# Cross attention on one Trainium2 core: the row order of the key and query stacks, and the weight columns that feed them

## The reference, cut to what matters

```python
qh = (layernorm(x) @ Wq + bq)      # 256 x 256, split into 16 heads of 16
kh = (ctx @ Wk + bk)
vh = (ctx @ Wv + bv)
attn = softmax(qh @ kh.T * scale)  # per sequence and head, 256 x 256
x = x + (attn @ vh) @ Wo + bo
```

## Time and profile before

| | |
|---|---|
| median of 3 runs | 2549.36 us |
| the profiled execution, its own time | 2551.32 us |
| its span | 2549.6 us |
| mean granted clock of PE | 0.945 of full |
| PE busy | 2233.4 us, 88% of the span |
| DVE / ACT / POOL busy | 1249.1 / 1044.1 / 690.6 us |
| DMA packets | 110,836, of them 95,256 under 2 KB |
| bytes moved | 164.30 MB |
| stack DMAs (lines 590 and 606) | 144 + 144 of 128 KB |
| L0x, L2x, L3x start at | 4.6, 1334.8, 2013.3 us |

### The profile page before, as it was taken

How to read it: one execution, slowest core, us unless ns; L and a number is a source line. 1 busy time by engine, 2 the same in 40 slices (tenths; PEclk the granted TensorE clock), 3 DMA queues, 4 the chain that set the end, 5 groups by cost and what they waited for, 6 DMA issues and landing times. The chain is left out here.

```text
span 2549.6 us, 43063 instructions
## 1 busy us (share of the span) xinstructions
PE 2233.4 (88%) x13610; PEld 1651.1 (65%) x13611; DVE 1249.1 (49%) x2762; ACT 1044.1 (41%) x2555; POOL 690.6 (27%) x684
## 2 busy tenths in 40 slices
PE   8998398668898999898898998999997599879998
PEld 4664398434465874466785664679996356558887
DVE  4664300379776229876434664100000466567864
ACT  1664133213565433466532663134443046544332
POOL 1000200337522436621541000320001410044443
PEclk8999699789999999999998998999998789999999
DMA  7761143110000000000007741133221476100001
GB/s 183 160 168 69 49 166 111 40 42 0 26 0 15 26 17 0 25 0 4 11 10 143 126 78 73 40 116 106 72 105 51 102 154 125 33 26 20 25 26 34
DMA packets 110836, 164.30 MB, mean 64 GB/s; under 512 B 15272, under 2 KB 95256, under 8 KB 105720
## 3 DMA queue, kind: packets, MB, share of 16 engines
q1 hardware_dynamic: 101712, 140.68, 21.6%
q0 software_dynamic: 7680, 20.98, 2.7%
q10 hardware_dynamic: 1320, 1.03, 0.2%
HBM read 114.96 MB, written 47.32 MB: 64 GB/s over the span
## 5 line engine op out<-in xcount | busy, mean ns | idle before, releaser
L1037 DVE TENSOR_REDUCE xa_mx<-ps 128x2 f32<-128x512 f32 x384 | 247.0, 686 | 103.0 <-PE ps L689 101.8
L141 PE MATMUL ps<-ones 128*128 128x384 f32 (+1 forms) x450 | 165.1, 496 | 100.9 <-DMA ex_rows<-rows_out,rows_back 39.0
L896 ACT ACTIVATE xn_tok<-ps 128x512 f32<-128x512 f32 x384 | 210.6, 602 | 52.2 <-PE ps L697 50.3
L1476 PEld LDWEIGHTS ps<-ex_xT,ex_w 128*128 128x128 f32 x1792 | 210.7, 194 | 7.3 <-issue 4.5
L1476 PE MATMUL ps<-ex_xT,ex_w 128*128 128x128 f32 x1792 | 211.3, 277 | 3.9 <-issue 3.9
L1483 PE MATMUL ps<-ex_w,ex_h 128*128 128x256 f32 x896 | 202.7, 379 | 0.0
L141 PEld LDWEIGHTS ps<-ones 128*128 128x128 f32 x450 | 90.8, 223 | 145.6 <-issue 52.1
L689 PE MATMUL ps<-xa_ks,xa_qs 48*128 48x256 f32 (+1 forms) x768 | 158.8, 328 | 27.4 <-DMA xa_qs<-x_queries 9.4
L2141 PE MATMUL ps<-lo_w,lp_hs 128*128 128x512 f32 x384 | 176.1, 610 | 4.8 <-ACT lp_hs L2189 2.8
L1483 PEld LDWEIGHTS ps<-ex_w,ex_h 128*128 128x128 f32 x896 | 166.1, 190 | 20.0
L689 PEld LDWEIGHTS ps<-xa_ks,xa_qs 48*128 48x128 f32 (+1 forms) x768 | 107.8, 197 | 101.7 <-DVE xa_mx L1037 53.0
(11 more groups left out here) (344 smaller groups left out, 5006.6 us busy)
## 6 DMA issues: line engine op xcount, KB each, us to landing
xa_ks<-x_keys SPq DMA_DIRECT2D x144, 128.0 KB
xa_qs<-x_queries SPq DMA_DIRECT2D x144, 128.0 KB, 4.3
ex_w<-in_L0f_w_dram SPq DMA_DIRECT2D x16, 1024.0 KB, 7.1
ex_w<-in_L2f_w_dram SPq DMA_DIRECT2D x16, 1024.0 KB, 6.9
x_keys<-xa_khl SPq DMA_DIRECT2D x24, 512.0 KB, 5.3
x_queries<-xa_qhl SPq DMA_DIRECT2D x24, 512.0 KB, 3.0
ex_stage<-rows_in POOLq DMA_DIRECT2D x64, 128.0 KB, 2.3
rows_out<-ex_rows SPq DMA_DIRECT2D x56, 128.0 KB, 1.7
```

The lines of the kernel that those rows point to most:

```text
L141: self.nc.tensor.matmul(self.ps[:, bank, 0:wide * P], self.ones[:], self.ones[:].unsqueeze(1).to_broadcast([P, wide, P]), start=True, stop ...
L896: nc.scalar.activation(pT[:, h % SLOTS].rearrange("p k q -> p (k q)"), c.ps[:, S_BANK + (HEADS * b + n) % 3], ACT.Exp).then_inc(exped.sem, 1)
L1037: nc.vector.tensor_reduce(mx[:, half, :, col], c.ps[:, M_BANK + h % 2].rearrange("p (t n) -> p t n", t=2), AX_X, ALU.max).then_inc(max_put ...
L1476: ins = nc.tensor.matmul(c.ps[:, f % 4, 0:P], w1[:, buf, k, f * P:(f + 1) * P], xT[:, k], start=(k == 0), stop=(k == KD - 1))
```

## The change

The features of keys and queries are put in another order, and with them the rows of the stacks.

- On the host `by_row` permutes the columns of `Wq` and `Wk` of all three layers, and the biases `bk` and `bq` of L2x: from (pair of heads, head of the pair, feature) to (head of the pair, feature, pair of heads). In DRAM the same feature of the eight heads of one parity then stands in eight neighbouring rows, 8 KB in one run.
- A stack DMA therefore reads 16 runs of 8 KB and writes 16 partitions with 8 KB each. Before, it did the same in 128 pieces of 1 KB.
- The 16 rows of one copy no longer lie on 16 neighbouring partitions but three apart: the copies are interleaved (rows 0, 3, 6 ..., rows 1, 4, 7 ..., rows 2, 5, 8 ...). The contraction is over the same 48 rows in another order.

Nothing else changes: every engine has the same instructions in the same order, with the same waits and the same bytes. Only the shape of the DMAs of lines 590 and 606 is another, 16 x 2048 floats in place of 16 x 8 x 256.

```diff
-                parts = dram["x_keys"][b].rearrange("(a g j r) t -> a j r g t", a=2, g=PAIRS, j=2)
+                parts = dram["x_keys"][b].rearrange("(a j r g) t -> a j r g t", a=2, g=PAIRS, j=2)
                 for j in range(2):
                     for n, part in enumerate((0, 0, 1)):
-                        at = 64 * j + HD * n
-                        sp.dma_start(ks[at:at + HD, b % K_BUFS].bitcast(F32), parts[part, j]
+                        at = 64 * j + n
+                        sp.dma_start(ks[at:at + 3 * HD - 2:3, b % K_BUFS].bitcast(F32), parts[part, j]
                                      ).then_inc(k_in[b % 3].sem, 16)
...
-                parts = dram["x_queries"][b].rearrange("(a g j r) t -> a j r g t", a=2, g=PAIRS, j=2)
+                parts = dram["x_queries"][b].rearrange("(a j r g) t -> a j r g t", a=2, g=PAIRS, j=2)
                 for j in range(2):
                     for n, part in enumerate((0, 1, 0)):
-                        at = 64 * j + HD * n
-                        sp.dma_start(qs[at:at + HD, b % Q_BUFS].bitcast(F32), parts[part, j]
+                        at = 64 * j + n
+                        sp.dma_start(qs[at:at + 3 * HD - 2:3, b % Q_BUFS].bitcast(F32), parts[part, j]
                                      ).then_inc(q_in[b % 2].sem, 16)
...
+    def by_row(w):
+
+        return w.reshape(w.shape[:-1] + (HEADS // 2, 2, HD)).swapaxes(-3, -2).swapaxes(-2, -1).reshape(w.shape)
+
     for tag, src in (("L0x_", "L0_xattn_"), ("L2x_", "L2_xattn_"), ("L3x_", "L3_xattn_")):
         for name in ("Wq", "Wk", "Wv", "Wo"):
-            o[tag + name.lower()] = _chunked(a[src + name])
-    o["L2x_wk"][KC[1], 1] = a["L2_xattn_bk"]
+            w = a[src + name]
+            o[tag + name.lower()] = _chunked(by_row(w) if name in ("Wq", "Wk") else w)
+    o["L2x_wk"][KC[1], 1] = by_row(a["L2_xattn_bk"])
...
-    o["L2x_qcol"] = a["L2_xattn_bq"].reshape(KD, P).T
+    o["L2x_qcol"] = by_row(a["L2_xattn_bq"]).reshape(KD, P).T
```

## The result

The changed kernel takes 2535.77 us in the median of six runs (2531.51 to 2537.15), the kernel before 2549.86 us beside it (2547.86 to 2559.96). The ratio is 0.9934 with a 95% interval from 0.9915 to 0.9954: faster by 14.1 us, or 0.66%. The forecast was 2526 us with a range from 2516 to 2540. The time lies in the range and the kernel is faster, as forecast, but by 14 us where 23.7 were expected.

A forecast was written before the change was run, and what follows sets the result against it. PE was taken to bound the kernel, waiting on stack transfers at each cross attention layer's start. Terms 9.4 + 9.6 + 2.7 + 2.0 = 23.7 us off 2551.32 gave 2527.6, as a median 2526 us, range 2516 to 2540.

The forecast's parts named there:

- Term A: PE's idle time before the first score of the three cross attention layers, expected gone in full: 9.4 us.
- Term B: Without idle time PE runs steps 0 to 2 of each cross attention layer at full clock, 5.5 us each: gain 9.6 us.
- The rate: Stack transfers were taken to flow at 205 GB/s, between 126 to 136 now and 279 that SP can issue.
- Term C: From step 3 to the first second scores, a shorter DRAM trip of the first maxima: 2.7 us, ends 0 and 4.1.
- Term D: PE's later waits on the maxima, 7.5 us in nine waits, partly go: 2 us, ends 0 and 7.5.
- R1: Rival, chance 0.07: the stack transfer rate does not rise, 134 GB/s stays and nothing moves: 2549 us.
- R2: Rival, chance 0.16: PE's clock falls in the lead-in even without idle time before it, Term B is lost: 2535 us.
- R3: Rival, chance 0.05: 8 KB pieces hold up the maxima, up to 2.6 us on each of 15 trips: 2567 us.
- the case given the most chance: The forecast itself, chance 0.72: all four terms gained in the cross attention layers, median 2526 us, 0.9% less.
- Packets: Sign in the changed kernel's profile: packets under 2 KB down by 36,864, to about 58,400.
- Rate "175 or more": Sign: 175 GB/s or more while only stacks run; if still 134, R1 holds.
- Step 3 after 5.5 us: Sign in each layer's lead-in: first score to step 3 near 5.5 us; if 8 or 9, R2 holds.

## Why the prediction came out as it did

**What bounds the kernel, and the rate as the cause: right.** The gain is in the three cross attention layers, 20.5 us in the profile. The undoing of the spread takes all of it away, and the spread alone brings all of it, so the cause is the spread of the rows. The way from the faster transfers to the time is shown only in part. The prediction adds the idle time (A) and the clock (B) as gains by themselves. With the slow transfers both could be had without any gain, in the kernel with the gap filled. They count only if the second stacks and the maxima move up too.

**The rate: mis-sized, and this is the step that failed first.** Taken was 205 GB/s, halfway to what SP could issue; it is 150 to 159. All three layers needed 175 to 183 for term A, so the sentence that the exact value matters little was wrong in the region where the value lay. The upper end moved as well: the text left an issue at 0.47 us and thought it might become shorter; it rose from 431 to 589 ns, or from 0.47 to 0.61 us with the gap behind it. In L0x, where mask rows go between the stacks, the issue alone would have held the rate at 177 GB/s, just below the 178 that term A needed there. The prediction's estimate from the port rule of the Trainium skill, "SBUF — State Buffer", Door 1, was 1.5 times today's rate. It was also too high: the measured factor is 1.17. The 1.5 comes from an average over the four busiest ports. In each of the three copies the busiest port has 3 rows in place of 4, and if that one sets the rate, the estimate is a factor of 1.33, still above the measured one.

**Term A**, expected 9.4 us: 3.9 us of the waits remained, so 5.5.

**Term B**, expected 9.6 us: from the first score to step 3 pass 5.52, 7.06 and 5.51 us, against the 5.5 that the text had worked out. In L0x and L3x it is right to 0.02 us. In L2x a wait of 1.69 us was left, the clock fell for a while, and 1.6 us were lost. Together 26.1 - 18.1 = 8.0 us.

**Term C**, expected 2.7 us: right in L2x (9.06 us where 9.1 was said) and in L3x (9.02), wrong in L0x. There the stretch became longer, 57.72 - 44.07 = 13.65 us against 12.0, by the wait for the second query stack. Together C lost 0.3 us. The step that failed is "would still be under way; I take half of 2.9": it priced the maxima's trip only and did not set the arrival of the second stacks themselves against a lead-in whose first steps became 3.5 us shorter. The trip itself did become shorter, 3.3 us in place of 5.3. Said generally, the question "what is late next" was answered for step 0 and not for the step after it.

**Term D**, expected 2 us: the waits on maxima fell by 4.1 us.

Sum of the four: 5.5 + 8.0 - 0.3 + 4.1 = 17.3 us of the 20.5. These terms count from the end of the filling matmuls, and in L2x that end came 1.7 us later after the layer's start than before. Counted from the start of each layer, the first second scores come 3.70, 2.70 and 5.05 us earlier, together 11.4, where A to C promised 21.7. Another 9.1 us were gained behind them (2.0, 5.3 and 1.8), where D promised 2.0. The second profile of the changed kernel has 13.5 and 7.9. So it is in part luck that the gain in the layers, 20.5, is close to the 23.7 forecast: the terms of the lead-in were too large and the one behind it too small. The gain behind the lead-in was not divided further among causes; the clock of the first sequence of L2x, 1.00 over 21 us from 1376 where it had been 0.86 in the 21 us from 1382, is a part that the text had only in its low end. Of the 20.5 us the other layers gave back 4.0 in that execution, 3.7 of them in the last stretch, at a granted clock of 0.95 in place of 0.96.

**The rivals.** R1 (the rate does not rise) is what happens when only the runs are made longer: 1 KB and 8 KB pieces flow alike, at 126 to 136 and 131 to 138 GB/s. With this the trace agrees with the Trainium skill, "DMA: Bandwidth & Descriptors", Specifications, which asks for pieces of at least 512 B for line rate. R2 (the clock falls in the lead-in anyway) is wrong: the 5.5 us to step 3 show it in L0x and L3x. The other sign named, four first scores in 0.51 us, is a weak one by itself. With the long runs alone and with the early context in the kernel before, the first scores took 0.50 or 0.51 us behind waits of 2.6 to 3.6 us, and step 3 still came only after 8.0 to 8.6 us. R3 (long pieces before the maxima) has its mechanism at most at a small price: 3.8 us more waits and 0.34% with neighbouring rows, where 39 us had been allowed; with spread rows the waits fell. The sign of the change was right, and the case given the most chance is the one that came, apart from its sizes.

**The checks named beforehand.** Packets: as said. Rate "175 or more": missed, 150 to 159. No wait before the first score: missed in all three. Four scores in 0.51 us: met. Step 3 after 5.5 us: met in two. Second scores 14.6 us behind the last filling matmul: missed, 17.8 us in L2x and 15.8 in L3x. Waits on the maxima at or below 7.5 us: met, 3.4. Three layers shorter by 11 to 34 us: met, 20.5. Other layers within 2 or 3 us: missed by 1 us.

## What to carry to other kernels

When a transfer fills few partitions, look first at which partitions they are; try them spread, and measure the issue time of the new shape along with its rate. A transfer that is waited for at the start of a pipeline has a successor: before the gain is booked, set the next transfer's arrival against the shortened work, since here a later wait took back part of it. Filling a gap so that the clock stays up pays only if what comes behind can be taken earlier; in this kernel it moved the same wait by some microseconds.

## What was not expected of the hardware

- The rate of a DMA from DRAM that fills 16 partitions hung on their spread and not on the length of the pieces: about 132 GB/s for neighbours, with 1 KB or 8 KB, 150 to 163 three apart, 169 to 177 for two of three copies two apart (161 to 176 in L0x over five profiles, where the issue is near the limit).
- The issue on SP grew from 431 to 589 ns with a step of three between partitions (600 ns with short pieces, 420 ns for long pieces on neighbours). In the kernel with two copies two apart and one on neighbours, the issues of all six DMAs took 0.48 to 0.59 us, those on neighbours too. Why is open.
- After PE had idled 2.9 us with the stacks on neighbours and 8 KB runs, its next four scores still took 0.51 us, and only those behind them were slower (1.36 us for the next four). In the kernel before, 2.85 us of idle time were followed by four scores in 0.80 us. So how soon the slower scores come behind an idle stretch differs between these profiles; why is open.
